# Two ways to take the inverse square root of a layer norm: one power on GpSimd, or a guess on VectorE and Newton steps on GpSimd

## The reference

```python
def _layernorm(x, axis=-1, eps=1e-05):
    m = jnp.mean(x, axis=axis, keepdims=True)
    v = jnp.var(x, axis=axis, keepdims=True)
    return (x - m) / jnp.sqrt(v + eps)
...
    x = x + _layernorm(_L0_attn_ref(_layernorm(x, axis=-1), ...), axis=-1)
    x = x + _layernorm(_L0_ffn_ref(_layernorm(x, axis=-1), ...), axis=-1)
```

## Time and profile before

| what | value |
|---|---|
| median of three runs | 1635.79 us (1635.27 to 1638.2) |
| the profiled execution, its own time | 1635.27 us |
| its span, from first to last instruction | 1633.5 us |
| PE busy | 1523.6 us, 93% of the span |
| DVE busy | 1223.4 us, 75% |
| ACT busy | 1113.0 us, 68% |
| POOL busy | 472.6 us, 29% |
| a turn in the steady part (414 to 577 us) | 163 us, of it PE 159.85, DVE 131.56, POOL 40.30 |
| mean granted TensorE clock | 0.983 |

### The profile page before, as it was taken

The page is one execution under the profiler, slowest core; times in us unless marked ns, Lnnn a source line. Parts: engine busy times, 40 slices in busy tenths (PEclk is TensorE's granted clock), DMA queues, the critical chain, the costliest instruction groups (busy, mean ns, idle before and its releaser), DMA issues.

```text
span 1633.5 us, 67801 instructions
## 1 busy us (share of the span) xinstructions
PE 1523.6 (93%) x28642; PEld 1184.4 (73%) x28642; DVE 1223.4 (75%) x3459; ACT 1113.0 (68%) x2053; POOL 472.6 (29%) x585
## 2 busy tenths in 40 slices
PE   5889989999999999999999999999999998899993
PEld 3337767787777777877777777777777776558992
DVE  7996658787878787888787878787877334644996
ACT  4437767777777777777777777777766766236881
POOL 4432020223122312231223122312201101564567
PEclk9999999999999999999999999999999999999996
DMA  3478675775564456444644564456424672425551
GB/s 85 143 191 219 170 174 110 178 179 144 114 153 103 118 113 152 101 123 110 153 102 117 115 152 98 119 116 147 97 54 102 124 211 68 119 89 152 156 171 51
DMA packets 489136, 212.10 MB, mean 130 GB/s; under 512 B 330663, under 2 KB 462436, under 8 KB 488832
## 3 DMA queue, kind: packets, MB, share of 16 engines
q1 hardware_dynamic: 474112, 165.74, 44.4%
q0 software_dynamic: 14720, 42.03, 7.5%
HBM read 105.73 MB, written 102.85 MB: 128 GB/s over the span
## 4 chain that ended last, share of the span: by engine, by line
PE 69%; DVE 18%; issue 4%; SPq 3%; DMA 2%; POOL 1%; ACT 1%; ACTq 0%; DVEq 0%; POOLq 0%
PE pv L867 13%; PE mix L822 11%; DVE mx L1380 10%; PE sc L845 8%; PE rel L874 7%; PE sc L847 7%; PE mix L824 6%; PE sc L839 4%; PE sc L1029 2%; PE sc L965 1%; PE pv L966 1%; POOL out_dram L1971 1%; PE rel L975 1%; DVE oS L1408 1%; PE mix L884 1%
## 5 line engine op out<-in xcount | busy, mean ns | idle before, releaser
L1121 ACT ACTIVATE w<-sc,escale 128x512 f32<-128x512 f32 x1024 | 686.2, 688 | 321.2 <-PE sc L847 183.2
L1380 DVE TENSOR_REDUCE mx<-mix 128x1 f32<-128x512 f32 x960 | 643.1, 683 | 213.4 <-PE mix L824 204.2
L822 PE MATMUL mix<-WE 128*32 128x512 f16 (+1 forms) x1968 | 386.4, 392 | 29.1 <-DVE mx L1380 19.3
L867 PE MATMUL pv<-w,shared_part 128*9 128x128 f32 x8192 | 373.0, 274 | 4.2 <-issue 4.0
L824 PE MATMUL mix<-Wn,WE 128*32 128x384 f16 (+3 forms) x1968 | 295.4, 304 | 0.3 <-issue 0.3
L845 PEld LDWEIGHTS sc<-shared_part,Wt 96*128 96x128 f16 x5120 | 223.2, 97 | 85.3 <-issue 31.3
L845 PE MATMUL sc<-shared_part,Wt 96*128 96x64 f16 x5120 | 258.8, 192 | 4.3 <-ACT w L1121 1.9
L867 PEld LDWEIGHTS pv<-w,shared_part 128*9 128x9 f32 x8192 | 205.5, 90 | 77.2 <-issue 47.8
L874 PE MATMUL rel<-w,shared_part 128*32 128x128 f32 x5120 | 258.3, 273 | 0.2 <-issue 0.2
L847 PE MATMUL sc<-shared_part 104*128 104x128 f16 x2560 | 248.7, 219 | 0.0
L1106 ACT ACTIVATE WE<-qp,hmask 128x256 f16<-128x256 f16 x500 | 215.7, 500 | 23.6 <-PE sc L824 23.6
(11 more groups left out here) (263 smaller groups left out, 1922.4 us busy)
## 6 DMA issues: line engine op xcount, KB each, us to landing
qm_d<-ks POOLq DMA_DIRECT2D x48, 512.0 KB, 4.9
shared_part<-qm_d SPq DMA_DIRECT2D x32, 768.0 KB
kt_d<-ks SPq DMA_DIRECT2D x48, 256.0 KB
shared_part<-kt_d SPq DMA_DIRECT2D x128, 96.0 KB
xs_d<-zrow SPq DMA_DIRECT2D x5, 2056.0 KB, 13.1
vs_d<-vst SPq DMA_DIRECT2D x16, 576.0 KB
shared_part<-vs_d SPq DMA_DIRECT2D x32, 288.0 KB
orl_d<-rel_s SPq DMA_DIRECT2D x512, 8.0 KB
```

Of the source, the lines that this page charges most:

```text
L822: nc.tensor.matmul(nat[rows, :], lq[:, rows], kn[b2][:, KEYS_AT[t]:KEYS_AT[t] + S], start=True, stop=False, skip_group_check=True)
L867: mm = nc.tensor.matmul(pv[b2][32 * g:32 * g + 9, P * hh:P * hh + P], VC[j][:, b2, 0 if near else 1, h, :], wt[:, :, b2, h, :], start=(j = ...
L1121: nc.scalar.activation(weights, products, ACT.Exp, scale=escale[:, 0:1]).then_inc(s["exp_done"], 1)
L1380: nc.vector.tensor_reduce(mx[:, k:k + 1], nat[:], AX.X, ALU.max).then_inc(s["mx_done"], 1)
```

## The change

`moments` no longer ends with one instruction of DVE, but with three: variance plus eps, halved, in one; a shift of its bits to the right by one; and the multiply and add on the bits that turn this into a guess of the root. The power on POOL gives way to `refine`: three Newton steps of four 128 x 4 instructions, each followed by a wait of POOL for that instruction's own semaphore. `normalize` waits for the 12th of them. The tile `power` and its memset go, a scratch tile `rtmp` comes. POOL's `root` no longer waits for `xn_done`. For the very last batch, DVE's own root now finds the guess already made by `moments`, so its 15 instructions become 12, and the separate halving goes. The other edits are counts of semaphores that follow from this.

```diff
-def root_guess_step(eng, k, half, root):
+def root_guess_step(eng, k, mean_var, half, root):
     if k == 0:
-        return eng.tensor_scalar(half[:], half[:], 0.5, None, ALU.mult)
+        return eng.tensor_scalar(half[:], mean_var[:, :, 1], EPS, 0.5, ALU.add, ALU.mult)
...
             ins.then_inc(s[step], 1)
-            dve.wait_ge(s[step], base + 2)
-            nc.vector.tensor_scalar(half[:], mean_var[:, :, 1], EPS, None, ALU.add).then_inc(s[step], 1)
+            for k in range(3):
+                dve.wait_ge(s[step], base + 2 + k)
+                root_guess_step(nc.vector, k, mean_var, half, rs).then_inc(s[step], 1)
...
             if tiles[0] == 0:
-                dve.wait_ge(s[root], roots + 1 + (LAST_ROOT_STEPS - 1) * max(0, roots + 1 - (4 * NP - 2)) * (root == "root2"))
+                dve.wait_ge(s[root], NEWTON_STEPS * (roots + 1))
...
-                for k in range(LAST_ROOT_STEPS):
+                for k in range(NEWTON_STEPS):
                     dve.wait_ge(s["root2"], base + k)
-                    if k < 3:
-                        root_guess_step(nc.vector, k, var2, rstd2).then_inc(s["root2"], 1)
-                    else:
-                        newton_step(nc.vector, k - 3, rstd2, var2, rtmp2, c15).then_inc(s["root2"], 1)
+                    newton_step(nc.vector, k, rstd2, var2, rtmp2, c15).then_inc(s["root2"], 1)
...
+        def refine(root, ve, tmp, name, n):
+            for k in range(NEWTON_STEPS):
+                newton_step(pool, k, root, ve, tmp, c15).then_inc(s[name], 1)
+                pool.wait_ge(s[name], NEWTON_STEPS * n + k + 1)
...
-            pool.wait_ge(s["xn_step"], 3 * c + 3)
-            at_least(pool, "xn_done", c)
-            pool.tensor_tensor(rstd[:], var[:], power[:], ALU.pow).then_inc(s["root"], 1)
+            pool.wait_ge(s["xn_step"], 5 * c + 5)
+            refine(rstd, var, rtmp, "root", c)
...
-            pool.wait_ge(s["ln_step"], 8 * c + 4 * (k + 1))
-            pool.tensor_tensor(rstd2[:], var2[:], power[:], ALU.pow).then_inc(s["root2"], 1)
+            pool.wait_ge(s["ln_step"], 12 * c + 6 * (k + 1))
+            refine(rstd2, var2, rtmp2, "root2", 2 * c + k)
...
-LAST_ROOT_STEPS = 3 + 12
+NEWTON_STEPS = 12
```

More of the change, by code:

```diff
@@ L145, in attention_phase @@
         a[n] for n in "qt_d qm_d qn_d kt_d vs_d rvp_d opv_d orl_d xs_d ysh_d x2T_d".split())
-    ident, sgu, sdn, ones, iota_e, owner, WE, c15, power = (a[n] for n in "ident sgu sdn ones iota_e owner WE c15 power".split())
+    ident, sgu, sdn, ones, iota_e, owner, WE, c15 = (a[n] for n in "ident sgu sdn ones iota_e owner WE c15".split())
     gate_up, down, out, we_ld, scat = a["gate_up"], a["down"], a["out"], a["moe_sem"]["we_ld"], a["moe_sem"]["scat"]
@@ L204, in attention_phase @@
     rstd = sb("rstd", [P, NT])
+    rtmp = sb("rtmp", [P, NT])
     xn = sb("xn", [P, NT, D])
@@ L363, in wait_for_bank @@
                 c = 2 * turn - what[1]
-                pe.wait_ge(*((s["ln_step"], 8 * c + 1), (s["x2T_ev"], c + 1), (s["lg_read"], c + 1), (s["cnt_read"], c + 1))[what[2]])
+                pe.wait_ge(*((s["ln_step"], 12 * c + 1), (s["x2T_ev"], c + 1), (s["lg_read"], c + 1), (s["cnt_read"], c + 1))[what[2]])
                 return
@@ L1290, in prep @@
                     dve.wait_ge(x_ld[b2], 16 * (n + 1))
-                moments(xt[b2], st, mv, var, rstd, 3 * c, "xn_step", step)
+                moments(xt[b2], st, mv, var, rstd, 5 * c, "xn_step", step)
             elif step == 2:
@@ L1398, in finish @@
             c = 2 * n + half
-            base = 8 * c
+            base = 12 * c
             if step == 0:
@@ L1426, in finish @@
             elif step == 10:
[L1427 removed]
+                dve.wait_ge(s["ln_step"], base + 7)
                 at_least(dve, scat, 64 * c)
@@ L1432, in finish @@
                     dve.wait_ge(s["x1_done"], c + 1)
-                moments(xs[:, :, HALF:HALF + D], st2, mv2, var2, rstd2, base + 5, "ln_step", step - 11)
+                moments(xs[:, :, HALF:HALF + D], st2, mv2, var2, rstd2, base + 7, "ln_step", step - 11)
             elif step == 13:
@@ L1624, in _ @@
             if u in (4, 5):
-                base = 4 * NP - 2 + LAST_ROOT_STEPS * (u - 4)
-                dve.wait_ge(s["ln_step"], 8 * (2 * last + 1) + 4 * (u - 3))
-                for k in range(LAST_ROOT_STEPS):
+                base = NEWTON_STEPS * (2 * (2 * last + 1) + u - 4)
+                dve.wait_ge(s["ln_step"], 12 * (2 * last + 1) + 6 * (u - 3))
+                for k in range(NEWTON_STEPS):
                     dve.wait_ge(s["root2"], base + k)
-                    if k < 3:
-                        root_guess_step(nc.vector, k, var2, rstd2).then_inc(s["root2"], 1)
-                    else:
-                        newton_step(nc.vector, k - 3, rstd2, var2, rtmp2, c15).then_inc(s["root2"], 1)
+                    newton_step(nc.vector, k, rstd2, var2, rtmp2, c15).then_inc(s["root2"], 1)
         place_tokens(last, 1, 0, mix[0])
@@ L1918, in _ @@
         pool.memset(c15[:], 1.5).then_inc(z, 1)
-        pool.memset(power[:], -0.5).then_inc(z, 1)
         zeros(QC[0])
-        pool.wait_ge(z, 2)
+        pool.wait_ge(z, 1)
         root(0, 0)
@@ L1991 @@
 ACT_HEADS = 4
-ZEROED_FIRST = 5 + E
+ZEROED_FIRST = 4 + E
 ZEROED = ZEROED_FIRST + 1
-LAST_ROOT_STEPS = 3 + 12
+NEWTON_STEPS = 12
 PLACE_STEPS = 27
```

1 line of the change is left out of this document (removed).

## The result

The changed kernel took 1658.39 us, the median of four runs (1654.56 to 1661.88). The kernel before took 1635.88 us beside it (1635.27 to 1638.2). The ratio is 1.0135, with a 95% interval from 1.0109 to 1.016. The profiled execution took 1658.59 us, 23.3 us more than that of the kernel before. So the change costs about twice the 11.6 us that were predicted.

A forecast was written before the change was run, and what follows sets the result against it. PE was taken to set the pace, DVE in places. Half 1 7.9, half 0 2.8, prologue 1.5, last batch -0.6 gave 11.6 us on 1635.27, so 1647 us; range for 8 in 10, 1640 to 1660.

The forecast's parts named there:

- Bounds and coupling: PE sets the pace, 69% of the chain of waits; DVE does in places (18%), POOL hardly (1%); PE and DVE trade banks.
- T: Time from the last guess instruction on DVE to POOL's root: 2.88 us, with 2.2 and 3.4 as low and high.
- The step of POOL: Each of 12 dependent instructions takes 0.15 us plus a 0.085 us gap: 2.74 us, and 0.14 for two handovers.
- Guess instructions: Two more DVE instructions per moments, 0.41 us; full cost at half 1's xs, about 0.4 us at half 0's y.
- Prep: Norm of a coming batch: root not late, guess instructions cost nothing in the turns; 5 us if DVE's cover is gone.
- rival C: DVE late beside prep's norms too, from lost cover or POOL's steps holding up DVE: 1652 to 1653 us, chance 10%.
- Prologue: DVE sets the pace; moments of two batches cost 1.5 us (0.8 to 3), as guess instructions may meet POOL's 2.12 us instruction.
- Last turn: Without row maxima DVE waits for the root directly; two roots each 2.1 us later are hidden, costing nothing.
- Last batch: One instruction fewer per norm, the halving of line 124: 0.6 us off the chain.
- A, hidden: PE's values work between banks absorbs DVE's lateness; only prologue and last batch show: 1635 to 1638 us, chance 10%.
- B: POOL's steps are long, 0.19 us each with a 0.17 us gap, so T is 4.3 us: 1669 us, chance 15%.
- sum of the high ends: Half 1 14.1, half 0 2.8, prologue 3.0, last batch -0.6: 19.3 us more, or 1654.6 us.

The follow-up runs named there:

- pool_only: Kernel before, power kept, with eight dependent 128 x 4 multiplies on POOL behind each power, DVE waiting for the last: 1686.98 us, ratio 1.0078.
- guess_only: Kernel before, power kept, with two more DVE instructions in each of the moments, writing a tile nobody reads: 1684.88 us, ratio 1.0060.
- steps8: Kernel after with 8 instead of 12 Newton instructions (two iterations instead of three): 1681.2 us, ratio 1.0053 to the kernel before.
- cover2: Kernel after with half 1's moments one slot earlier and y's first normalize at slot 32 instead of 30, xs's normalize unmoved: 1649.9 us, ratio 1.0063.
- second pair of traces: Kernels before and after, both unchanged, traced again on one other chip: 1641.46 us before and 1657.2 us after, ratio 1.0106.
- cover: Kernel after with half 1's moments one slot earlier and first normalizes later (y 30 to 32, xs 41 to 42): 1690.14 us, ratio 1.0092.
- pool_free: Kernel before with eight 128 x 4 multiplies on POOL behind each power, independent of each other, DVE waiting for the last: 1676.24 us against 1673.77.

## Why the prediction was right about the direction and short in size

**Bounds and coupling: right.** The engine averages hid the matter and the local rows showed it. DVE waits for POOL at half 1, PE waits for DVE two banks on. Put T = 3.44 into the prediction's own steps for y: the root comes at 516.48 + 0.17 + 0.41 + 3.44 = 520.50, the row maximum behind it ends at 520.50 + 0.53 + 0.68 = 521.71, and PE starts at about 521.76 instead of 520.30: 1.46 us late. Measured were 1.45 in the rows above and 1.50 at the mean. For xs the same working gives 0.41 + 0.56 = 0.97 us; measured 0.97. pool_only alone falls where this puts it, and so do guess_only and steps8 at y. At xs those two gave 0.25 us, where the prediction had 0.41.

**The step of POOL: mis-sized, and this is the step that failed.** The prediction took 0.15 us for an instruction, between a memset of 91 ns and a select of 188 ns, and 0.085 us for the gap. The gap was right (0.078). The instruction was 0.199 us, just above the near upper bound, so T became 3.44 us and not 2.88. That is 0.56 us more in T. At y, where PE's slack was used up already, it adds 0.56 us to the delay, and at xs, which was just without a stall at 2.88, 0.56 us too: 1.12 us in a turn, 6.7 over six (measured: 2.47 - 1.31 = 1.16, or 7.0). It is the larger part of what was missing. The two handovers took 0.19 us (522.23 to 522.38 and 525.63 to 525.67) where 0.14 were put; the 0.10 us behind that was read at 517.77, where DVE came from its row maxima and did not wait for POOL, so the row gave no price for them. Neither neighbour was an arithmetic instruction with two input tiles, and the choice of the middle had no row of its own.

**Guess instructions: right at y, too dear at half 1's xs.** 0.41 us at half 0's y and at half 1's y. At half 1's xs the prediction let them cost their full 0.41 us, but by themselves they cost 0.25 us; the stall hides that difference in the kernel after. Half 1's 2.47 us are 0.66 for the guess, which stays in guess_only and steps8 and nearly so in cover2, and 1.81 for the stall, which cover2 takes away. Over six turns this is 4.0 and 10.9 us.

**Prep: right.** It cost nothing in the turns, and neither half of rival C occurred there.

**Prologue: the collision was right, the 1.5 us were luck.** The first pair of traces shows 2.0 us at the first finish, the second -1.2 us, so this term does not repeat. What repeats lies earlier: at DVE's normalize of 73.96 the distance is 1.7 us in the first pair and 2.2 in the second, and waits behind it change it. A guess instruction did meet POOL's long one (timeline of POOL, then of DVE, in the kernel after; compare):

```profile
44.81 2.12 POOL L1856 TENSOR_TENSOR ks<-WE,ks 128x1024 f16<-128x1024 f32 x1
46.89 0.60 POOL L1822 CAST qs<-WE 128x512 f16<-128x512 f32 x1
```

```profile
45.13 1.83 DVE L123 TENSOR_SCALAR var<-mv 128x4 f32<-128x4 f32 x1
46.99 0.52 DVE L125 TENSOR_SCALAR rstd<-var 128x4 int32<-128x4 int32 x1
```

L123 ends at 46.96 and L125 at 47.51, where POOL's two instructions end at 46.93 and 47.49. Two of DVE's three were held up, where before it was one. The Trainium skill, SBUF — State Buffer, section "SBUF: two separate sides", has a port pair that the two engines share and that the first to start keeps for its whole instruction; it says this of VectorE instructions in a two-port mode or with two SBUF inputs. The ends, 0.03 and 0.02 us apart, agree with such a lock; in which mode these two ran no run here shows.

**Last turn: costed at nothing; 5.0 us in one pair of traces, next to nothing in the other.** The two long roots did stand open (timeline of DVE, then PE, in the kernel after; compare):

```profile
1338.34 1.12 DVE L1284 TENSOR_SCALAR xs<-xs,mv,rstd 128x128 f32<-128x128 f32 x4 [3.43 <-POOL rstd L137]
```

```profile
1339.61 0.63 PE L749 MATMUL mix<-ident,xs 128*128 128x128 f32 x4 [0.24 <-DVE xs L1284]
```

The wait is 3.43 us, and PE now waits for the result, 0.24 us. The 10 us between 1312.62 and 1323.58 that hid the root before are gone: PE takes the result up at a distance of 16.0 us, where 20.2 stood at the start of the turn. Later in the turn the reciprocals of line 1409 wait for a transfer:

```profile
1373.63 3.39 DVE L1409 RECIPROCAL oS<-oS 128x128 f32<-128x128 f32 x4 [18.02 <-DMA xr<-in_L_attn_x_dram]
```

The same row was at 1351.01 before, with a wait of 11.23 us: the distance is 22.6 us there, 20.2 at the start of the turn and 25.2 at the last batch's first instruction. That the late roots delay what SP issues in this turn fits these rows. But the second pair of traces speaks against the roots alone: there DVE falls back at the same norms of this turn in the same way, from 20.9 us at y's moments to 26.2 at xs's first normalize, and the distance is 20.9 us again at the last batch. The last turn and the last batch together added only 0.4 us. No experiment left the last turn's roots alone, so how the 5.0 us of the first pair come about stays open.

**Last batch: -1.9 us, predicted -0.6.** Between the instructions at 1412.42 and 1420.19 the distance falls by 0.1 us and to the one at 1437.51 by 1.8. The two halvings that went explain some 0.5 us of it; the rest, among the work of the shared expert, was not followed.

**The rivals.** A, hidden, fell: PE waits 21 us more. B was the nearest, since a step was 0.199 us and not 0.15; but its gap of 0.17 us wasn't there. With T at 3.44 the measured time lies between the forecast and B, at the upper end of the range. The sum of the high ends was 1654.6 us, 3.8 us below the measured median; the range reached 1660 by a margin that no term stood behind. That 1658.39 fell inside it was partly luck.

## What to carry to other kernels

When one instruction of a slow kind is split into a chain of cheap ones on an engine, price the chain by its dependent steps from start to start, and bound the step by the nearest row with as many operands, not by a memset. Then find the one place where the consumer stands in the queue of an engine that feeds the critical one; there the stall less the slack between two buffers is what it costs, each time. Such a stall can be moved away by the order of the consumer's work (cover2), but the instructions added to a full queue remain, and a use that is moved too far is waited for by the next engine (cover).

## What the runs showed of the hardware

- POOL's power on 128 x 4 takes 1.01 us, a multiply of that shape 0.20. Independent ones start 0.15 us apart, dependent ones 0.277.
- In a stall of 5.6 us PE stood idle from 385.2 us on, and its granted clock was at 0.50 from about 387.3 to 394.1. Around half 1's stalls of 2.25 us it stayed at 1.00.
- The same kernel before took 1636, 1641 and 1674 us on different chips, more than the change costs. In pool_free's trace, on a chip of the last kind, only some 10 of about 40 us had arisen by the end of the seventh turn. What makes the rest was not looked for.
